# A twelve-stage decoder: expert weights asked for in the router stages, a third weight buffer, and a paged attention in one block instead of two

## What is computed

```python
q = (x @ wq).reshape(B, T, H, D)              # 16 heads of 16
lat = x @ w_down                              # 256 -> 128
k = (lat @ wk_up).reshape(B, T, H, D)
v = (lat @ wv_up).reshape(B, T, H, D)
q = _apply_rope(q, cos, sin)
k = _apply_rope(k, cos, sin)
allowed = pages[None, :] <= pages[:, None]    # pages of 64 tokens
scores = jnp.where(allowed[None, None], jnp.einsum('bqhd,bkhd->bhqk', q, k) * scale, min)
out = jnp.einsum('bhqk,bkhd->bqhd', softmax(scores), v).reshape(B, T, E) @ wo
```

```python
expert_id = jnp.argmax(jnp.einsum('bsh,he->bse', x, wr) + br, axis=-1)
h = gelu(jnp.einsum('bsh,ehf->ebsf', x, w1) + b1)     # 256 -> 1024
y = jnp.einsum('ebsf,efh->ebsh', h, w2) + b2          # 1024 -> 256
out = jnp.einsum('ebsh,bse->bsh', y, one_hot(expert_id))
```

## Time and profile before

| | |
|---|---|
| median of three runs | 2941.3 us (2937.02 to 2941.55) |
| the profiled execution | 2937.35 us, its span 2935.5 us |
| granted clock of PE, mean | 0.898 of full speed |
| PE busy | 2414.5 us (82%), 13995 instructions |
| DVE, ACT, POOL busy | 1503.2, 857.4, 488.7 us |
| paged attention | 554 to about 995 us |
| first router, first experts | 1070 to 1090, 1090 to about 1336 us |
| second router, second experts | about 1909 to 1991, from 1991.8 us |
| weights of the second experts | 8 requests of 2180 KB on SP's queue |

### The profile page before, as it was taken

How to read it: one execution, slowest core, us unless ns; L and a number is a source line. 1 busy time by engine, 2 the same in 40 slices (tenths; PEclk the granted TensorE clock), 3 DMA queues, 4 the chain that set the end, 5 groups by cost and what they waited for, 6 DMA issues and landing times. The chain is left out here.

```text
span 2935.5 us, 35285 instructions
## 1 busy us (share of the span) xinstructions
PE 2414.5 (82%) x13995; PEld 1669.9 (57%) x14003; DVE 1503.2 (51%) x2550; ACT 857.4 (29%) x1223; POOL 488.7 (17%) x395
## 2 busy tenths in 40 slices
PE   5876756747888968975999998937999599999888
PEld 3665643422222767763666666735777467777674
DVE  8996966448775340014564565462111345545543
ACT  1111656412556212213433233201111222212132
POOL 3332320130000012311001000102221120000010
PEclk8898978966999979997999999857999799999979
DMA  3002000052441024532322221013222110000000
GB/s 106 0 1 100 2 30 1 11 130 44 67 70 30 13 75 179 212 135 88 92 64 89 61 65 58 8 56 97 96 97 87 68 52 17 17 12 17 1 31 29
DMA packets 71009, 176.71 MB, mean 60 GB/s; under 512 B 16478, under 2 KB 36447, under 8 KB 67280
## 3 DMA queue, kind: packets, MB, share of 16 engines
q1 hardware_dynamic: 60480, 122.60, 15.0%
q0 software_dynamic: 8208, 50.01, 4.8%
q10 hardware_dynamic: 2176, 2.10, 0.2%
HBM read 149.04 MB, written 25.43 MB: 59 GB/s over the span
## 5 line engine op out<-in xcount | busy, mean ns | idle before, releaser
L1575 PE MATMUL L_ffn_h_ps<-L_ffn_xgT,L_ffn_w 128*128 128x512 f32 (+2 forms) x992 | 241.7, 402 | 19.2 <-DMA L_ffn_w<-in_L_ffn_w,group_rows 16.9
L2215 PE MATMUL L_attn_X<-xT,L_attn_w 128*128 128x512 f32 x512 | 227.4, 597 | 0.0
L1587 PE MATMUL L_ffn_y_ps<-L_ffn_w,L_ffn_h 128*128 128x256 f32 x1008 | 223.0, 381 | 4.0 <-ACT L_ffn_h L1612 3.9
L1575 PEld LDWEIGHTS L_ffn_h_ps<-L_ffn_xgT,L_ffn_w 128*128 128x128 f32 x992 | 160.6, 199 | 101.2 <-issue 65.8
L530 DVE TENSOR_REDUCE L_attn_neg<-L_attn_R 128x1 f32<-128x512 f32 (+3 forms) x304 | 187.5, 658 | 54.8 <-PE L_attn_R L407 53.3
L1612 ACT ACTIVATE L_ffn_h<-L_ffn_h_ps,L_ffn_w 128x640 f32<-128x640 f32 (+2 forms) x184 | 101.5, 552 | 388.9 <-PE L_ffn_h_ps L1575 359.1
L1587 PEld LDWEIGHTS L_ffn_y_ps<-L_ffn_w,L_ffn_h 128*128 128x128 f32 x1008 | 190.2, 191 | 32.2 <-ACT L_ffn_h L1612 7.9
L407 PE MATMUL L_attn_R<-L_attn_K,L_attn_Q 104*128 104x512 bf16 (+3 forms) x384 | 119.7, 364 | 83.1 <-DVE L_attn_K L524 48.5
L496 ACT ACTIVATE L_attn_probs<-L_attn_S 128x1024 f32<-128x1024 f32 (+1 forms) x192 | 147.3, 812 | 79.5 <-PE L_attn_S L453 78.9
L2215 PEld LDWEIGHTS L_attn_X<-xT,L_attn_w 128*128 128x128 f32 x512 | 95.2, 191 | 110.1 <-issue 108.3
L1633 DVE COPY L_ffn_xgT<-L_ffn_t_ps 128x256 f32<-128x256 f32 x63 | 24.6, 421 | 246.9 <-PE L_ffn_t_ps L1562 246.9
(11 more groups left out here) (529 smaller groups left out, 4795.7 us busy)
## 6 DMA issues: line engine op xcount, KB each, us to landing
L_ffn_w<-in_L_ffn_w SPq DMA_DIRECT2D x8, 2180.0 KB
L_attn_bc<-decays SPq DMA_DIRECT2D x32, 512.0 KB, 6.5
L_attn_w<-in_L_attn_w SPq DMA_DIRECT2D x16, 640.0 KB, 3.9
L_attn_bp<-decays SPq DMA_DIRECT2D x32, 256.0 KB, 7.0
L_attn_Q<-L_attn_q_parts SPq DMA_DIRECT2D x48, 128.0 KB, 4.9
L_attn_K<-L_attn_k_parts SPq DMA_DIRECT2D x48, 128.0 KB, 7.4
L_attn_w<-in_L_attn_w SPq DMA_DIRECT2D x16, 384.0 KB, 3.1
token_outputs<-zero SPq DMA_DIRECT2D x1, 4096.0 KB, 20.7
```

Source lines behind the costliest of these rows:

```text
L1575: ins = nc.tensor.matmul(h_ps[f % 2][:, lo // CW, 0:hi - lo], w1[u][:, kt, f * P:(f + 1) * P], xgT[u][:, kt, lo:hi], start=kt == 0, stop=k ...
L1587: ins = nc.tensor.matmul(y_ps[k % 2][:], h[:, f, t * P:(t + 1) * P], w2[u][:, f, :], start=f == 0, stop=f == FT - 1)
L2215: ins = nc.tensor.matmul(x[:, c * CW:(c + 1) * CW], w[1 - par][:, kt, r, :], xT[:, kt, b * T + c * CW:b * T + (c + 1) * CW], start=kt == 0 ...
```

## The change

Four edits.

1. The paged attention is one block. The projections' functions are called at the head of each engine's queue. The loop over batches is written out. `Q` and `K` exist from the start; `full`, `rot`, `rest` and `latT` lie in `oT`, and the probabilities lie in the room of the projection weights. The PSUM tiles `S` are `Y[1]`, and `R`, `O` and `Tp` are `Y[0]`.
2. Page rows, and with them the three rows of ones, come as bf16 bits from DRAM straight into all slots (six requests at the head of the projections). DVE's memsets and casts are gone.
3. SP asks for stacks 0, 1 and 2 in the second batch, each behind a store.
4. Expert weights are an object made before the router. In the first router POOL asks for group 0's weights as soon as `group_rows` is written; there are three buffers, so a group's weights are asked for three groups ahead; at the head of the stage the token rows of groups 0 and 1 are asked for before the weights of groups 1 and 2. In the second router SP asks for the weights of groups 0 and 1 behind the early loads; that stage keeps two buffers.

```diff
+        def projections_on_sync(sp):
+            for par in range(SLOTS):
+                for stack, rows, src in ((Q, slice(KP, KM), "page_q"), (K, slice(KP, KS), "page_k")):
+                    sp.dma_start(stack[rows, par, :, :].rearrange("p j t -> p (j t)").bitcast(I32), A[src]).then_inc(pages_loaded, 16)
+            for b in range(B):
+                for r in range(NR):
+
+                    sp.wait_ge(part_done[2], b * NR + r + 1)
+                    for g in range(2):
+                        it = b * NG + r % 2 * 2 + g
+                        sp.dma_start(parts_dram[r // 2][:, it:it + 1, :, :].rearrange("c i p t -> p (c i) t"),
+                                     parts[g * G * DH:(g + 1) * G * DH, r % 2, :, :]).then_inc(stored[r % 2], 16)
+                    if b == 1 and r < SLOTS:
+                        sp.wait_ge(stored[r // 2], 16 * NR)
+                        load(sp, r)
...
+        @block.tensor
+        def _(pe):
+            projections_on_tensor(pe)
+            pe.wait_ge(pages_loaded, 16 * 2 * SLOTS)
+            pe.wait_ge(rot_done, B * NR - 1)
+            pe.wait_ge(v_copied, B)
+            for n in range(NU):
+                row_max(pe, 0, n)
...
+                pe.wait_ge(neg_in, it * 48 + 48)
+                if it == 0:
+                    pe.wait_ge(rot_done, B * NR)
...
+                                act.wait_ge(pv_mm, it * NQ + LAST[c] + 1)
+                                if it + c == 0:
+                                    act.wait_ge(part_done[2], B * NR)
...
-                for par in range(SLOTS):
-                    nc.vector.memset(K[KP:KS, par, :, :], 1.0).then_inc(const_set, 1)
...
-                for par in range(SLOTS):
-                    nc.vector.tensor_copy(Q[KP:KM, par, :, :], over(page_q[KP:KM, :], G)).then_inc(const_set, 1)
-                    nc.vector.tensor_copy(K[KP:KM, par, :, :], over(page_k[KP:KM, :], G)).then_inc(const_set, 1)
...
+    def load(self, eng, g):
+        n, u = self.order[g][0], g % self.count
+        if self.dynamic:
+            at = bass.IndirectOffsetOnAxis(self.core.group_rows[:, n:n + 1], 0)
+            self.nc.gpsimd.indirect_dma_start(self.tiles[u][:], None, self.src, at).then_inc(self.loaded[u], 16)
+        else:
+            eng.dma_start(self.tiles[u][:], self.src[n * P:(n + 1) * P, :]).then_inc(self.loaded[u], 16)
...
             for g in range(2):
-                if dynamic:
-                    weights(g)
                 take(g)
+            if dynamic:
+                for g in range(1, NB):
+                    weights.load(pool, g)
...
-                if dynamic and g + 2 < groups:
-                    weights(g + 2)
+                if dynamic and g + NB < groups:
+                    weights.load(pool, g + NB)
...
+        @block.gpsimd
+        def _(pool):
+            pool.wait_ge(owners_known, 1)
+            weights.load(pool, 0)
...
             following.load(sp)
+            for g in range(weights.count):
+                weights.load(sp, g)
             sp.wait_ge(core.zeroed, 16)
```

More of the change, by code:

```diff
@@ L1475, with __init__, there, sparse_experts_stage @@
 NT = N // P
-def sparse_experts_stage(nc, core, name, func, choices, order, dynamic, keys, first_row):
-    A = core.A
+class ExpertWeights:
+    def __init__(self, nc, ctx, core, name, order, buffers, dynamic):
+        self.nc, self.core, self.order, self.dynamic, self.count = nc, core, order, dynamic, buffers
+        self.src = core.A[f"{name}_w"]
+        self.tiles = [ctx.enter_context(nc.sbuf_tensor(f"{name}_w{u}", [P, self.src.shape[-1]], F32)) for u in range(buffers)]
+        self.loaded = [nc.alloc_semaphore(f"{name}_w{u}_loaded") for u in range(buffers)]
+    def load(self, eng, g):
[5 more added lines that the diff above has]
+            eng.dma_start(self.tiles[u][:], self.src[n * P:(n + 1) * P, :]).then_inc(self.loaded[u], 16)
+    def there(self, eng, g):
+        eng.wait_ge(self.loaded[g % self.count], 16 * (g // self.count + 1))
+def sparse_experts_stage(nc, core, name, func, choices, order, weights, keys, first_row):
     F = 1024
@@ L1500, in sparse_experts_stage @@
     with Mem(nc, name) as m:
-        w = [m.sb(f"w{u}", [P, WW]) for u in range(2)]
+        w, NB, dynamic = weights.tiles, weights.count, weights.dynamic
         w1 = [x[:, 0:KT * F].rearrange("p (k n) -> p k n", k=KT) for x in w]
@@ L1535, in _ @@
         def _(sp):
-            def weights(g):
-                if not dynamic:
-                    n = order[g][0]
-                    sp.dma_start(w[g % 2][:], A[f"{name}_w"][n * P:(n + 1) * P, :]).then_inc(w_loaded[g % 2], 16)
-            for u in range(2):
-                weights(u)
-            for g in range(2, groups):
-                sp.wait_ge(sem["y_copied"], before[g - 1])
-                weights(g)
+            if not dynamic:
+                for g in range(NB, groups):
+                    sp.wait_ge(sem["y_copied"], before[g - NB + 1])
+                    weights.load(sp, g)
             all_put(sp)
@@ L1606, in _ @@
                 n = size[g] * P
[L1607 removed]
+                weights.there(act, g)
                 if g:
@@ L1669, in _ @@
         def _(pool):
-            def weights(g):
-                n = order[g][0]
-                at = bass.IndirectOffsetOnAxis(core.group_rows[:, n:n + 1], 0)
-                nc.gpsimd.indirect_dma_start(w[g % 2][:], None, A[f"{name}_w"], at).then_inc(w_loaded[g % 2], 16)
             def take(g):
@@ L1888, with top2_router_stage @@
 SHIFTS = [26, 22, 18, 14, 10, 6, 2, 0]
-def top2_router_stage(nc, core, following, early):
+def top2_router_stage(nc, core, following, early, weights):
     w = early.tiles
@@ L2029, in top1_experts_stage @@
 def top1_experts_stage(nc, core, keys, router):
-    top1_router_stage(nc, core, keys.early, router)
     pair = lambda j: (j, 2 * P * j, 2)
```

727 lines of the change are left out of this document (353 added, 374 removed).

## The result

The changed kernel took 2859.3 us, the median of four runs (2855.2 to 2863.8), against 2941.4 (2937.0 to 2944.3): ratio 0.9722, 95% interval 0.970 to 0.9745. The prediction was 2860.0. The sum of the terms was 80.

The account below looks back on a forecast made before the run. It took TensorE, busy most of the time, to be held by waits at the touched places; 38 + 32 + 10 = 80 us off the profiled 2937.35 gave 2857.4, predicted as 2860 for the median, range 2847 to 2882.

Parts of the forecast that it names:

- Paged attention, 38: Projections to row maxima: first row-maximum product at 631 in place of 669.13 us, set by stack 0's landing; gain 38 us.
- rival C: Projections: stores' landing gates ScalarE, GpSimd and VectorE, so each stack's 5.5 us of requests delays them; 16.5 us less, chance 0.05.
- A: Paged attention: stacks land late, like the crowded 13.5 us group or worse; gain 5 or 10 us less, chance 0.17.
- signs of being wrong: Row maxima past 637, steady-part token-row waits, pairs at 8.9 us, or a stage after the touched ones over 1 us longer.
- First experts, start, 6.0: First experts' head: weights asked for at 1081.98, landed by 1092.3; first product at 1098.2 against 1104.21, gain 6.0 us.
- lower bound of 3.5: First experts' start: gain of 3.5 us if token rows land 4 us after their request.
- The sign I gave: First experts' head: first product within 16 us of the owners' table being written.
- The rival on the shared port: First router: VectorE holds the port, GpSimd-requested weights move only from 1089.3; start gain about 4.5, chance 1 in 5.
- Waits and clock of the first experts, 16.9 + 7.9 + 1.5 = 26.3: First experts: seven weight waits go (16.9 us), slower products behind them (7.9), and part of the first group's slowness (1.5).
- B: First experts: token rows queued behind weights, or the clock, take back the weights' gain; 14 us less, chance 0.10.
- D: Rival whose claim the text does not state; apparently chance 0.02, and excluded from the cases counted as faster.
- Second experts, 10: Second experts' head: weights asked for in the router; token-row wait shrinks by 8.6 us, first group's clock gives 1.4.

Follow-up runs that it names:

- e4: Changed kernel with three memsets and six casts done again by VectorE before the row maxima, which wait for them; stacks stay early: 2891.0 us, ratio 0.9809.
- e0: The changed kernel itself, unedited, run again for a second profile: 2855.8 us, ratio 0.9726.
- e6: Changed kernel with no weights asked for in either router; both experts ask at their heads, token rows first, three buffers stay: 2876.6 us, ratio 0.979.
- e8: Changed kernel whose first router's GpSimd asks for 128 KB of token rows, not 2180 KB of weights; group 0's weights asked at the experts' head: 2863.1 us.
- e11: e10 with only group 0's up weights (1024 KB) asked for in the first router, the rest at the experts' head: 2860.3 us, ratio 0.9726.
- e5: Changed kernel with two weight buffers in the first experts in place of three: 2888.8 us, ratio 0.9841.
- e9: Changed kernel with 24 unread extra TensorE products in the second experts, between the keys' products and the first turn of token rows: 2864.6 us, ratio 0.9754.
- e10: Changed kernel with 7 unread extra TensorE products in the second experts ahead of the first turn: 2852.6 us, ratio 0.9701.

## Why the prediction was right, and where it was not

**Paged attention, 38.** Measured 39.2 and 39.5 between VectorE's last projection operation and the first row maximum, and stack 0 decides, as written. Two sizes under that number were off and cancelled: the twelve requests of stack 0 took 8.0 us (4.94 + 3.04), not 5.5; and the product followed the last of them by 5.3 us, not 8.6, in step with the landing (0.13 to 0.14 us behind it in all eleven executions with changed attention but without e4's casts). The first row maximum came out 1 us earlier for both. The projections themselves were not delayed: VectorE stood the same 2.30 us before its last round, so rival C didn't occur, nor did A: stack 0's last K landed 5.6 us after its request, not 13.5. One of the signs of being wrong did show in the first profile, the attention behind its first row maximum 4.8 us longer than before; the same program without them (e0) took that sign away.

**First experts, start, 6.0.** This is the step that failed: it says that the first weights "landed at 1092.3" and charges nothing for the router's end. They did land in time (9.2 us after the ask), but the end of the router's block waited for them: the keys' products begin 3.6 us after the token-row table and not 1.2. Inside the stage the gain is 5.5; net it is 3.2 (22.2 us from the owners' table to the first up product before, 19.0 after), below my lower bound of 3.5. The sign I gave, "the first product of the first experts within 16 us of the table's write", was missed by 3 us for this reason, and e6, e8 and e11 show it. The rival on the shared port is not what happened: from 1052 to 1054 VectorE was busy 1.93 of 2 us, and the DMA engines were busy at 0.74 with GpSimd's request. It landed in 9.2 us, and the loads of the steady part took 8.5 to 9.6. The Trainium skill ("SBUF — State Buffer", SBUF: two separate sides) says that a request of GpSimd's starves while a VectorE operation holds the port that both share. This request didn't starve; whether VectorE's operations of up to 1.2 us in the router hold that port, no run shows.

**Waits and clock of the first experts, 16.9 + 7.9 + 1.5 = 26.3.** Measured 26.5 and 26.1. All seven pairs take 7.12 us, the granted clock is 1.00 throughout; token rows are never late, so neither B nor D. e5 gives the seven waits back, with 10.0 us of slower pairs where I had 7.9 from the trace.

**Second experts, 10.** Measured 7.7 and 7.9 up to the first up product. The wait fell to 3.21 and 2.79 (I had taken 2). The size that was off is the "some 2 us" in which token rows land when alone: those of the fifth request, the last that TensorE waits for, landed 4.4 us after it was asked for, 3.1 us after its issue had ended. Of the 1.4 for a warmer first group nothing came in the first execution (20.48 against 20.15) and 0.8 in the second (19.37). e9 shows that the clock can stay up there, e10 that filling the wait doesn't do it.

**Sum.** 76.4 by the pieces, 80 predicted: the attention gave 1.2 more, the first experts 2.5 less (32 predicted, 29.5 measured), the second 2.3 less. By the pieces the median would be 2941.4 - 76.4 = 2865; it was 2859.3. That the number comes within 1 us of 2860 is luck within an execution's spread: the profiled execution was 74.3 below that of before, the second 81.7.

## What to carry to other kernels

A stage boundary is a wait for transfers too: what GpSimd asks for just ahead of it can hold up everybody behind it, so ask earlier, for less, or after the boundary. Where two things are late by nearly the same, here VectorE's casts and the stacks, taking one away shows little, 8 or 12 us of 39; both have to go. In a long run of products a wait of 2 to 3 us can cost clock as well: here 16.9 us of waits went with 7.9 us of slower products, and 17.1 with 10.0, so half as much again is to be counted.

## What the runs showed of the hardware

- The end of a block waited for GpSimd's transfer: 3.54 to 4.3 us from the last table to the next stage with 2180 KB under way, 0.86 us from the landing in six of six executions; 1.2 us from the table with 128 KB or 1024 KB (landed) or none.
- Granted clock: behind most TensorE waits of 2 to 3 us the next products ran partly at 1.2 GHz (pairs of 8.6 to 8.9 us against 7.12, five of seven in the kernel before and six of seven in e5; a first group of 19.0 to 20.5 against 17.5). With 10.5 us of products in place of the wait it stayed at 2.4 GHz, with 3.2 us of them it did not (19.23).
- The same 128x128 cast on VectorE took 0.23 us at 655.38 in the kernel before and 2.07 us at 630.94 in the changed one, where a GpSimd subtraction lay over it. In all twelve executions of the changed attention it took 2.07 us and ended 0.08 us behind that subtraction's end.
- Places that no edit touches differ between executions: the changed attention behind its first row maximum took 325.8 to 332.5 us in twelve of them (both ends are the changed kernel itself), and the stretch between the two experts 645.8 to 655.3 in fourteen.
